# Cross-attention with a routed feed-forward: the softmax sums inverted small and then spread, squares and part of the context split on GpSimd, and exponentials moved ahead in ScalarE's order

## What is computed

```python
xn = layernorm(x)
q = rms_norm(xn @ q_w.T + q_b) * norm_q_w                   # 112 rows, 16 heads of 32
k_img = rms_norm(ctx[:257] @ k_img_w.T + b) * norm_k_img_w  # image part of the context
k     = rms_norm(ctx[257:] @ k_w.T + b) * norm_k_w          # text part, 118 rows
x = x + o(softmax(q k_img.T / sqrt(32)) v_img + softmax(q k.T / sqrt(32)) v)
x = x + top2_of_8_experts(layernorm(x))                     # 512 -> 1024 -> 1024 -> 512, gelu
```

## Time and profile before

| what | value |
|---|---|
| median of 3 runs | 930.0 us (927.8 to 933.55) |
| the profiled execution | 931.23 us |
| its span, first to last instruction | 929.4 us |
| mean granted PE clock | 0.931 of full speed |
| busy in the span: PE / DVE / ACT / POOL | 773.7 / 588.3 / 505.8 / 69.6 us |

### The profile page before, as it was taken

The page is one execution under the profiler, slowest core; times in us unless marked ns, Lnnn a source line. Parts: engine busy times, 40 slices in busy tenths (PEclk is TensorE's granted clock), DMA queues, the critical chain, the costliest instruction groups (busy, mean ns, idle before and its releaser), DMA issues.

```text
span 929.4 us, 17429 instructions
## 1 busy us (share of the span) xinstructions
PE 773.7 (83%) x6238; PEld 676.3 (73%) x6238; DVE 588.3 (63%) x1001; ACT 505.8 (54%) x1154; POOL 69.6 (7%) x94
## 2 busy tenths in 40 slices
PE   2888989898989898773079999999999999999930
PEld 2566666666666666552079999999999999999920
DVE  5466767676767676746136767676767676767634
ACT  4566767676767676751044545454545555555510
POOL 2100000000000000000600000000000000000014
PEclk9989999999999999855579999999999999999975
DMA  7850102010202000407625656565656565656568
GB/s 245 312 210 1 64 11 64 12 64 11 63 12 65 11 22 11 158 11 260 204 86 187 233 184 236 185 235 183 236 184 236 184 236 184 234 183 237 181 226 259
DMA packets 33982, 137.53 MB, mean 148 GB/s; under 512 B 3712, under 2 KB 3728, under 8 KB 22928
## 3 DMA queue, kind: packets, MB, share of 16 engines
q1 hardware_dynamic: 31200, 129.23, 40.0%
q0 software_dynamic: 2736, 7.69, 2.9%
HBM read 115.36 MB, written 21.54 MB: 147 GB/s over the span
## 4 chain that ended last, share of the span: by engine, by line
PE 68%; DVE 9%; ACT 9%; issue 7%; DMA 3%; POOL 2%; SPq 0%; POOLq 0%; ACTq 0%; DVEq 0%
PE tiles L960 7%; PE tiles L962 7%; PE tiles L961 7%; PE scores L1191 4%; PE scores L1193 4%; PE scores L1192 4%; PE ptb L1051 3%; PE pvb L962 3%; PE pvb L961 3%; PE pvb L960 3%; PE ptb L962 3%; PE ptb L961 3%; PE ptb L960 3%; PE scores L1042 2%; ACT scr L543 2%
## 5 line engine op out<-in xcount | busy, mean ns | idle before, releaser
L776 DVE TENSOR_TENSOR w<-scr,w 128x2048 fp32r<-128x2048 f32 x76 | 174.2, 2292 | 84.6 <-ACT w L568 84.6
L568 ACT ACTIVATE w<-scr 128x2048 fp32r<-128x2048 f32 x76 | 144.8, 1907 | 63.2 <-PE scores L1193 59.3
L960 PE MATMUL tiles<-c,w 128*128 128x256 f32 (+1 forms) x272 | 83.0, 305 | 22.1 <-DVE c L672 17.5
L1051 PE MATMUL ptb<-ident,scr 112*128 112x112 f32 x384 | 64.4, 279 | 25.9 <-ACT scr L553 25.9
L960 PE MATMUL tiles<-w 128*128 128x256 f32 x288 | 81.5, 283 | 0.0
L961 PE MATMUL tiles<-w 128*128 128x256 f32 x288 | 81.5, 283 | 0.0
L962 PE MATMUL tiles<-w 128*128 128x256 f32 x288 | 81.5, 283 | 0.0
L961 PE MATMUL tiles<-c,w 128*128 128x256 f32 (+1 forms) x272 | 79.9, 294 | 0.0
L962 PE MATMUL tiles<-c,w 128*128 128x256 f32 (+1 forms) x272 | 79.9, 294 | 0.0
L1051 PEld LDWEIGHTS ptb<-ident,scr 112*128 112x128 f32 x384 | 44.1, 149 | 48.9 <-ACT scr L545 35.1
L553 ACT ACTIVATE scr<-ptb 128x336 f32<-128x336 f32 x128 | 59.9, 468 | 26.9 <-PE ptb L1051 26.9
(11 more groups left out here) (212 smaller groups left out, 2120.9 us busy)
## 6 DMA issues: line engine op xcount, KB each, us to landing
scr<-in_dram SPq DMA_DIRECT2D x86, 1024.0 KB, 4.8
slots_d<-xr SPq DMA_DIRECT2D x3, 2048.0 KB, 17.5
scr<-in_dram SPq DMA_DIRECT2D x8, 750.0 KB, 4.9
scr<-slots_d SPq DMA_DIRECT2D x10, 512.0 KB, 4.6
slots_d<-scr SPq DMA_DIRECT2D x9, 512.0 KB, 3.8
xn<-in_dram SPq DMA_DIRECT2D x10, 256.0 KB, 4.7
xb<-in_dram SPq DMA_DIRECT2D x8, 224.0 KB, 4.9
xr<-in_dram SPq DMA_DIRECT2D x8, 224.0 KB, 2.5
```

The lines of the kernel that those rows point to most:

```text
L568: act.activation(EH[slot], raw[slot], ACT.Copy).then_inc(S["eh_done"], 1)
L776: dve.tensor_tensor(EL[slot], raw[slot], EH[slot].bitcast(F32), ALU.subtract).then_inc(S["el_done"], 1)
L960: pe.matmul(out, wh, xh, start=start, stop=False)
L1051: mm = pe.transpose(ptb[:, t * L:(t + 1) * L], probs[0:L, h % 4, t * P:(t + 1) * P], ident[0:L, 0:L])
```

## The change

The reciprocal now runs on the 8 sums themselves, and a copy spreads the results over 32 columns each, with a wait (`inverted`) between the two. All squares go from ACT to POOL, which reads them from the biased copies in SBUF (`kn`, `qn`) after the tile is freed. The high half of context part 1 goes from ACT at h = 2 to POOL, behind its first layer norm power; `ch_done` becomes two semaphores. The low half of part 1 on DVE goes from h = 3 to h = 6. In ACT's steps with h % 4 == 0 the exponentials now stand ahead of the stage.

```diff
@@ -133,7 +133,7 @@
         msb, rr = sb("msb", [P, 4]), sb("rr", [P, 4])
         nmax, sums = sb("nmax", [P, 2, 4, 2]), sb("sums", [P, 2, 2, 4])
         vx = sb("vx", [P, 2, D])
-        rx = sb("rx", [P, 2, 4, HD])
+        rsum, rx = sb("rsum", [P, 2, 4]), sb("rx", [P, 2, 4, HD])
         rbc, pvn, af = sb("rbc", [P, 2 * L]), sb("pvn", [P, 2 * L]), sb("af", [P, L])
         rms = sb("rms", [P, TOK])
         xlT = sb("xlT", [P, NC, B])
...
@@ -277,7 +277,7 @@


             act.wait_ge(S["c_in"], 16 * n)
-            act.activation(c_part(cH)[i], cr[:, :, PARTS[i]], ACT.Copy).then_inc(S["ch_done"], 1)
+            act.activation(c_part(cH)[i], cr[:, :, PARTS[i]], ACT.Copy).then_inc(S[("ch0_done", "ch1_done")[i]], 1)

         @block.sync
         def _(sp):
@@ -303,7 +303,8 @@
                 if has_prep(b):

                     if b < LAST - 1:
-                        sp.wait_ge(S["ch_done"], 2 * (b + 2))
+                        sp.wait_ge(S["ch0_done"], b + 2)
+                        sp.wait_ge(S["ch1_done"], b + 2)
                         sp.wait_ge(S["cl_done"], 2 * (b + 2))
                         sp.dma_start(cr, ctxT[b + 2]).then_inc(S["c_in"], 16)
                         sp.wait_ge(S["xn_done"], b + 2)
@@ -431,12 +432,33 @@
                 pool.wait_ge(S[tag + "_var"], b_count)
                 pool.tensor_tensor(rs[0:L, :], ve[0:L, :], mhalf[0:L, 0:1], ALU.pow).then_inc(S[tag + "_rstd"], 1)

+            def square(name, b, p):
+                taken(pool, name, b)
+                if name == "q":
+                    to, of = sq[:, :, 0:L], qn[:, 1 - p, :, :]
+                elif name == "kx":
+                    to, of = sq[:, :, L + IMG:TOK], kn[1 - p][:, :, IMG:KEYS]
+                else:
+                    c = int(name[1])
+                    to, of = sq[:, c, L:L + IMG], kn[1 - p][:, c, 0:IMG]
+                pool.tensor_tensor(to, of, of, ALU.mult).then_inc(S["squares"], 1)
             def body(b, p):
                 if has_prep(b):
                     rstd(b + 2, mv1, ve1, rs1, "ln1")
+                    if not fixed(b, -1):
+                        pool.wait_ge(S["c_in"], 16 * (b + 2))
+                        taken(pool, "v2", b)
+                        pool.tensor_copy(c_part(cH)[1], cr[:, :, PARTS[1]]).then_inc(S["ch1_done"], 1)
+                    if not fixed(b, -1):
+                        pool.wait_ge(tile_ready[tile_use("ms", b - 1)[0]], tile_use("ms", b - 1)[1] + 1)
+                    square("k0", b, p)
                 if has_tail(b):
                     rstd(b, mv2, ve2, rs2, "ln2")
                 if has_prep(b):
+                    for name in ("k1", "k2", "q", "kx", "k3"):
+                        square(name, b, p)

                     taken(pool, "ms", b)
                     pool.tensor_tensor(rr[:, :], msb[:, :], mhalf[:, :], ALU.pow).then_inc(S["r_done"], 1)
@@ -493,10 +515,6 @@
                     rows = P if t < 2 else TAIL
                     act.wait_ge(tile_ready[bank], cnt + 1)
                     act.activation(vn[p if t == 2 else 1 - p][0:rows, t, :], tiles[0:rows, bank, :], ACT.Copy).then_inc(tile_free[bank], 1)
-                if name == "q":
-
-                    taken(act, "q", b)
-                    act.activation(sq[:, :, 0:L], qn[:, 1 - p, :, :], ACT.Square).then_inc(S["squares"], 1)
                 if name in ("qt", "kt"):

                     rows = L if name == "qt" else TXT
@@ -507,16 +525,12 @@
                     act.wait_ge(tile_ready[bank], cnt + 1)
                     c = int(name[1])
                     bias = vec[:, V_KIB, c:c + 1]
-                    act.activation(sq[:, c, L:L + IMG], tiles[:, bank, 0:IMG], ACT.Square, bias=bias).then_inc(S["squares"], 1)
                     act.activation(kn[1 - p][:, c, 0:IMG], tiles[:, bank, 0:IMG], ACT.Identity, bias=bias).then_inc(tile_free[bank], 1)
                 if name == "rb":
                     act.wait_ge(tile_ready[bank], cnt + 1)
                     if not fixed(b, -1):
                         act.wait_ge(S["k_done"], NC * (b + 1))
                     act.activation(rms[:, :], tiles[:, bank, 0:TOK], ACT.Copy).then_inc(tile_free[bank], 1)
-                if name == "kx":
-                    taken(act, "kx", b)
-                    act.activation(sq[:, :, L + IMG:TOK], kn[1 - p][:, :, IMG:KEYS], ACT.Square).then_inc(S["squares"], 1)

             def split_keys(b, p, c):

@@ -597,13 +611,11 @@
                         split_keys(b, p, KEYS_HIGH_AT[h])
                     if h == 0 and has_prep(b) and not fixed(b, -1):
                         split_ctx(act, b + 2, 0)
+                    if h % 4 == 0 and has_heads(b):
+                        weigh(b, p, h)
                     for name in STAGE_AT[h]:
                         if has(name, b):
                             stage(name, b, p)
-                    if h % 4 == 0 and has_heads(b):
-                        weigh(b, p, h)
-                    if h == 2 and has_prep(b) and not fixed(b, -1):
-                        split_ctx(act, b + 2, 1)
                     if fixed(b, DONE) and h == 3:
                         for pc in range(3):
                             convert(0, pc)
@@ -668,7 +680,7 @@
             dve.tensor_tensor(vbias[:, :], vec[:, V_VB, :], vec[:, V_VIB, :], ALU.add).then_inc(S["vbias_done"], 1)

             def split_ctx_low(n, i):
-                dve.wait_ge(S["ch_done"], 2 * n - 1 + i)
+                dve.wait_ge(S[("ch0_done", "ch1_done")[i]], n)
                 dve.tensor_tensor(c_part(cL)[i], cr[:, :, PARTS[i]], c_part(cH)[i].bitcast(F32), ALU.subtract).then_inc(S["cl_done"], 1)

             def ln_stats(count, src, st, mv, tag):
@@ -758,7 +770,9 @@
                 dve.wait_ge(S["exp_done"], NH * b + 4 * g + 4)
                 if not (fixed(b, 0) and g < 1):
                     dve.wait_ge(S["pv_ready"], NC * b + g)
-                dve.reciprocal(rx[0:L], sums[0:L, g % 2, :, :].unsqueeze(3).to_broadcast([L, 2, 4, HD])).then_inc(S["rsum_done"], 1)
+                dve.reciprocal(rsum[0:L], sums[0:L, g % 2, :, :]).then_inc(S["inverted"], 1)
+                dve.wait_ge(S["inverted"], NC * b + g + 1)
+                dve.tensor_copy(rx[0:L], rsum[0:L].unsqueeze(3).to_broadcast([L, 2, 4, HD])).then_inc(S["rsum_done"], 1)

             def attended(b, g):

@@ -807,8 +821,8 @@
                         normalise_keys(p if step else 1 - p, c)
                     if h in KEYS_LOW_AT and has_heads(b):
                         split_keys_low(b, p, KEYS_LOW_AT[h])
-                    if h in (1, 3) and has_prep(b) and not fixed(b, -1):
-                        split_ctx_low(b + 2, h // 2)
+                    if h in (1, 6) and has_prep(b) and not fixed(b, -1):
+                        split_ctx_low(b + 2, h // 5)
                     if h == 2 and has_tail(b):
                         attended(b - 1, 3)
                     if h == 3 and has_tail(b):
```

4 lines of the change are left out of this document (2 added, 2 removed).

## The result

| what | before | changed |
|---|---|---|
| median of 4 runs each | 929.16 us (927.8 to 933.55) | 949.01 us (946.2 to 951.51) |
| the profiled execution, its span | 931.23, 929.4 us | 948.53, 946.5 us |
| busy PE / DVE / ACT / POOL | 773.7 / 588.3 / 505.8 / 69.6 us | 780.7 / 558.7 / 484.6 / 107.7 us |
| mean granted PE clock | 0.931 | 0.923 |

The ratio is 1.0184, 95% interval 1.0154 to 1.0214: the changed kernel is slower by 1.8%, forecast were 944 us and a range of 928 to 951. DVE and ACT have 29.6 and 21.2 us less to do, POOL has 38.1 more, and PE has the same instructions and is busy 7.0 longer; yet the time rises by more than that. So it is to be looked for in waits, body by body. The table gives the distance in us between the first score matmuls (h = 0) of neighbouring bodies; the first column is where that of body 0 starts.

A forecast was written before the change was run, and what follows sets the result against it. Each steady body was PE's work plus 5.46 us of PE standing. Bodies 1 to 5 +13.0 and clock +4.5, body 6 -2.0, body 0 -1.5: +14.0 on 931.2 gives 945.2, median 944, range 928 to 951.

The forecast's parts named there:

- The stand: Bodies 1 to 5: DVE's second layer norm waits for the late x1 store, PE stands 3.5 us, +2.15 us a body.
- Prologue and body 0: Prologue 0, late squares against ScalarE's relief; body 0 -1.5 us, from its score group that waits longer for ACT.
- Body 7: Last attention body: its waits are not for the reciprocal or the squares, so 0.
- What the rest gains a body: Body 6, without the stand: -1.63 before head 8, -0.81 at head 8, +0.45 for squares on POOL, -2.0 in all.
- The clock: Behind PE's stand in bodies 1 to 5 the granted clock falls: 0.9 us a body, bounds 0 and 1.7.
- B: Rival: the stand in bodies 1 to 5 is there but the clock holds, 939.5 us; chance 0.20.
- The exponentials' order: ACT's exponentials first: PE's 0.32 us wait at 248.54 goes, and the 0.81 at head 8 if DVE's maxima are on time.
- The reciprocal: On DVE ahead of the low context part: k0's 0.48 us wait goes once a body; DVE sheds 38 us busy time.
- The squares: On POOL, slower kx and k3 delay DVE's additions: 0.45 us a body, bounds 0 and 0.75; early squares relieve ACT.
- A: Rival: the store is no obstacle, bodies 1 to 6 gain 2.0 us each and body 0 1.5, 916.5 us; chance 0.12.
- C: Rival: POOL's kx square and DVE's two-input work contend, 0.65 us a body, 948.5 us; chance 0.10.
- D: Rival: it cancels; POOL's squares cost nothing, store lands sooner, clock holds, -5 in all, 925 us; chance 0.08.

The follow-up runs named there:

- store-first kernel: Changed kernel with SP issuing the x1 store ahead of the context load in the bodies that have both: 918.63 us, ratio to before 0.9875.
- the kernel with the move alone: Kernel before with only the low half of context part 1 on DVE moved from h = 3 to h = 6: 952.57 us, ratio 1.0224.

## Why the prediction came out as it did

Sign, mechanism and most of the size were right. In the profiled executions +17.3 us were measured, +14.0 forecast; between the medians it is +19.9, of which 0.8 is that the kernel before ran at 929.2 and not 930.0. By stretch, in us of span:

| stretch | forecast | measured |
|---|---|---|
| prologue and body 0, up to body 1 | -1.5 | 90.74 - 92.62 = -1.9 |
| bodies 1 to 5 | +17.5 | 254.70 - 232.26 = +22.4 |
| body 6 | -2.0 | 44.57 - 46.46 = -1.9 |
| body 7 and all behind it | 0 | 556.5 - 558.1 = -1.6 |

- **The stand.** DVE 28.4/5 = 5.7 us against 6.0, the landing 4.9 against 5.2, SP's three issues 0.87 apart against 0.90, PE 16.4/5 = 3.3 against 3.5. A queue's behaviour seen in one other place of the same trace (body 0, three transfers in a row) was the right price; the median of the store was not.
- **Prologue and body 0: luck.** The prologue was put at 0 and took 0.7 more (47.94 against 47.21), body 0 at -1.5 and took 2.6 less; the two misses nearly cancel.
- **Body 7.** Put at 0, and -1.6 was measured. The store, issued 11.4 us behind the body's first score group in both kernels, landed after 5.4 instead of 6.4, DVE stood 0.98 instead of 1.98 for it, and the expert loop starts 1.55 sooner behind that score group. Why it landed sooner stays open.
- **What the rest gains a body.** Forecast -2.0 (1.63 + 0.81 - 0.45), measured by the store-first kernel 44.54 - 46.46 = -1.9.
- **What the stand costs a body without the clock.** Forecast 2.15 plus the 1.63 and 0.81 it swallows, 4.6; measured 49.29 - 44.54 = 4.75.
- **The clock: the term that was mis-sized.** Forecast 0.9 a body: 1.7 us of work lost behind a stand, 0.8 of it hidden. Measured 1.65 a body; 5 x 0.75 = 3.8 of the 4.9 us by which bodies 1 to 5 were missed. The step "a stand of 3.5 us should do the same" as one of 1.96 was right for body 1 (1.7 lost) and wrong for bodies 2 to 5 (3.4 lost each). And less was hidden than was taken: the 1.7 of body 1 cost 1.2. The average lay just under my upper bound of 1.7, bodies 3 to 5 above it. The length of the stand, on which my argument against B rested, does not order the losses: stands of 3.2 to 4.6 us lost 1.7 each in the kernel with the move alone.
- **The parts inside the -1.9.** The exponentials' order, 0.74 a body by its own test, was forecast well. The reciprocal, 0.48 forecast, gave 0.28, since k1's wait grew by nearly what k0's fell, mostly by a collision that I had not in the sum. The squares, which I had put at a small gain with the early ones counted in, cost 0.47: the late pair 0.52 against my 0.45, but for another reason in the main. I had GpSimd slow and serial; the waiting for it is 0.14, and 0.38 is the collision of k3's square with a DVE addition. The early squares gained nothing. Moving the low half, which I had only as a danger, removes a wait of 1.5 us on DVE and is worth 0.6 a body once the store is first. So the forecast of -2.0 hit -1.9 with two of its terms off and one left out, which is luck in part. The parts undone one at a time come to 0.74+0.28-0.47-0.12+0.6 = 1.0; the other 0.9 of the gain shows only when several of them stand together, and no run says which.
- **Busy time.** DVE's fell by 29.6 us and not 38. The reciprocal gave 39.8; a's low part took 4.0 back, the first addition 2.8, the layer norm of x 1.1, and three more groups 1.5. ACT's fell by 21.2 and not 25 (the terms of 3.6 a body come to 3.7), POOL's rose by 38.1 against 40.
- **Rivals.** A, the store no obstacle: fell, but its number, 916.5, is what the kernel does when the store is made no obstacle (918.6). B, the clock holds: the opposite was the case. C, the two engines in each other's way: its 948.5 is nearest to the measured 949.0, and the collision is real, about 3 us as against 4.5, with k3's square in place of kx's. But most of it lay within what I had already charged to GpSimd's speed; what lifted the time above 944 was the clock. That its number fits is luck. D fell with the landing of 4.9; its own terms come to -5.7, not -5.

## What to carry to other kernels

In this kernel a DMA that an engine waits for was only as early as what stood ahead of it in SP's queue: when the last reader of a buffer is moved, look at which reload waits for that reader, and at what stands in the queue behind the reload. Issue what is due soonest first; here one store moved ahead of one load turned 1.8% slower into 1.3% faster. And test the parts of a bundle one by one: in this one the order of the exponentials was worth most, and the squares on another engine less than nothing.
